# Moving all 32 low-half subtractions of the weight split to GpSimd in a scan-plus-experts kernel

## What is computed

```python
xn = _layernorm(x)
x = x + attn(xn, A, W_delta, delta_bias, W_B, W_C) + ffn(xn, W1, b1, W2, b2, Wr, br)
# attn: delta = softplus(xn W_delta + bias); per step of L = 2048, per (d, n) of 256 x 16:
#   h = exp(delta A) h + (exp(delta A) - 1) / A * B_t * x_t ;  y = sum_n h C_t
# ffn: 8 experts, the best 2 of each token: gelu(xn W1[e] + b1[e]) W2[e] + b2[e], weighted
```

## Time and profile before

| | |
|---|---|
| median of 3 runs | 1374.65 us (1370.88 to 1374.74) |
| the profiled execution's own time | 1372.12 us |
| its span, first to last instruction | 1370.4 us |
| mean granted TensorE clock | 0.949 |
| busy: PE, DVE, ACT, POOL | 1199.7, 1048.8, 860.1, 841.5 us |

### The profile page before, as it was taken

One profiled execution on the slowest core, in us unless ns is written; L12 is line 12 of the kernel. 1 busy time (PEld: TensorE's weight loads), 2 busy tenths in 40 slices (PEclk: granted clock), 3 DMA queues, 4 the chain that ended last, 5 costly groups with the idle time before them and its releaser, 6 DMA issues. The chain is left out here.

```text
span 1370.4 us, 22272 instructions
## 1 busy us (share of the span) xinstructions
PE 1199.7 (88%) x7674; PEld 734.0 (54%) x7674; DVE 1048.8 (77%) x1413; ACT 860.1 (63%) x1422; POOL 841.5 (61%) x603
## 2 busy tenths in 40 slices
PE   1567767566999989999999999999999999999896
PEld 0432323223566656666666666666666666666552
DVE  6865889885777877867777767778777787777878
ACT  3645666655577557586767666675776857676521
POOL 2628989861647556566565757666575666656552
PEclk9558898988999999999999999999999999999999
DMA  6596667664343343343442443434534334334324
GB/s 207 194 267 193 231 218 243 204 246 143 83 107 109 115 113 113 103 115 110 137 118 84 131 128 92 123 111 122 127 93 132 113 98 130 113 108 111 84 47 142
DMA packets 87386, 186.95 MB, mean 136 GB/s; under 512 B 12784, under 2 KB 64880, under 8 KB 77168
## 3 DMA queue, kind: packets, MB, share of 16 engines
q1 hardware_dynamic: 69280, 163.19, 36.4%
q0 software_dynamic: 18000, 22.42, 9.8%
HBM read 135.48 MB, written 57.96 MB: 141 GB/s over the span
## 5 line engine op out<-in xcount | busy, mean ns | idle before, releaser
L921 POOL TENSOR_TENSOR ax<-ax,x 128x512 f32<-128x512 f32 x256 | 335.4, 1313 | 387.7 <-ACT ax L821 386.2
L1134 PE MATMUL bank<-k_xT,k_WB 128*128 128x512 f16 x1536 | 390.7, 392 | 102.5 <-DVE hb L1024 92.4
L1011 DVE TENSOR_TENSOR bank<-ax,bank 128x512 f32<-128x512 f32 x256 | 177.5, 693 | 281.7 <-PE bank L1134 246.4
L1134 PE MATMUL bank<-k_xT,k_WC 128*128 128x512 f16 x1536 | 386.5, 389 | 0.8 <-DVE ysum L1045 0.8
L1134 PEld LDWEIGHTS bank<-k_xT,k_WB 128*128 128x128 f16 x1536 | 146.0, 100 | 269.6 <-DVE hb L1024 118.4
L1134 PEld LDWEIGHTS bank<-k_xT,k_WC 128*128 128x128 f16 x1536 | 154.0, 100 | 194.0 <-issue 20.6
L1024 DVE TENSOR_TENSOR_SCAN hb<-aexp,state,bank 128x512 f32<-128x512 f32 x192 | 243.9, 1270 | 0.0
L814 ACT ACTIVATE aexp<-k_dcur,k_A 128x512 f32<-128x512 f32 x256 | 180.7, 711 | 59.4 <-DVE hb L1024 54.9
L1183 PE MATMUL bank<-stage,k_x 128*128 128x256 f16 x1872 | 217.1, 273 | 0.0
L1183 PEld LDWEIGHTS bank<-stage,k_x 128*128 128x128 f16 x1872 | 183.2, 98 | 37.8
L1036 DVE SCALAR_TENSOR_TENSOR bank<-hb,k_rA,bank 128x512 f32<-128x512 f32 x240 | 179.1, 746 | 1.7
(11 more groups left out here) (139 smaller groups left out, 1223.9 us busy)
## 6 DMA issues: line engine op xcount, KB each, us to landing
k_x<-wsplit SPq DMA_DIRECT2D x78, 1024.0 KB, 4.7
stage<-in_W SPq DMA_DIRECT2D x32, 512.0 KB, 5.2
wsplit<-stage SPq DMA_DIRECT2D x32, 512.0 KB, 3.2
xs<-k_zero SPq DMA_DIRECT2D x1, 10140.0 KB, 44.5
stage<-xs SPq DMA_DIRECT2D x39, 260.0 KB, 5.3
stage<-in_b SPq DMA_DIRECT2D x39, 128.0 KB
k_x<-in_x SPq DMA_DIRECT2D x4, 1024.0 KB, 9.8
stB<-in_WBT SPq DMA_DIRECT2D x8, 512.0 KB, 4.7
```

Of the source, the lines that this page charges most:

```text
L921: nc.gpsimd.tensor_tensor(ax[:, g % MR], ax[:, g % MR], x32[:, hf], ALU.mult).then_inc(ax_done, 1)
L1011: v.tensor_tensor(bank, ax[:, g % MR], bank, ALU.mult).then_inc(ux_done, 1)
L1134: ins = mm(bank[:], W[:, a, kc, n, hf * P:(hf + 1) * P], xT[:, c, b, kc, :], start=(k == 1), stop=(k == 3 * KC))
```

## The change

DVE no longer subtracts. POOL's `low_piece` takes every k instead of the even ones, each in tile `piece_step(k) + 4`. For an odd piece that is one tile number later than DVE had it. The two semaphores for "low half done" become one, and SP waits for its count.

```diff
-    p_lo = [sem("p_lo_pool"), sem("p_lo_dve")]
+    p_lo = sem("p_lo")
...
             if k >= W_BUF:
-                sp.wait_ge(p_lo[k % 2], (k - W_BUF) // 2 + 1)
+                sp.wait_ge(p_lo, k - W_BUF + 1)
...
         def store_piece(k):
-            sp.wait_ge(p_lo[k % 2], k // 2 + 1)
+            sp.wait_ge(p_lo, k + 1)
...
             nc.gpsimd.tensor_tensor(whl[:, k % HL_BUF, 1, :], wst[:, k % W_BUF, :], whl[:, k % HL_BUF, 0, :],
-                                    ALU.subtract).then_inc(p_lo[0], 1)
+                                    ALU.subtract).then_inc(p_lo, 1)
...
-            for k in range(0, SPLITS, 2):
+            for k in range(SPLITS):
                 if piece_step(k) + 4 == g:
                     low_piece(k)
...
-        def low_piece(k):
-            dve.wait_ge(p_hi, k + 1)
-            v.tensor_tensor(whl[:, k % HL_BUF, 1, :], wst[:, k % W_BUF, :], whl[:, k % HL_BUF, 0, :],
-                            ALU.subtract).then_inc(p_lo[1], 1)
...
-            for k in range(1, SPLITS, 2):
-                if piece_step(k) + 3 == g:
-                    low_piece(k)
             hc_op(g)
```

## The result

| | before | after |
|---|---|---|
| median | 1374.7 us (1370.88 to 1375.65, 4 runs) | 1388.03 us (1387.57 to 1389.3, 4 runs) |
| profiled execution, its span | 1372.12, 1370.4 us | 1387.66, 1385.9 us |
| first scatter starts | 107.80 us | 109.41 us |
| subtraction of piece 30 starts | 287.92 us | 307.94 us |
| last subtraction ends | 298.61 us | 313.38 us |

The changed kernel takes 1.0104 times as long (95% interval 1.0083 to 1.0124): it is 13 us slower. The forecast was 1389 us.

A forecast was written before the change was run, and what follows sets the result against it. POOL was taken to bound the piece stage: 31.4 us added less 9.8 and 2.6 put piece 30 at 306.9 us and the stage end 13.8 us later. With 0.3 for stores, 14 us on 1374.65 gave 1389 us, range 1382 to 1402.

The forecast's parts named there:

- POOL leads the stage: From first scatter to last subtraction, POOL sets the pace until its subtraction of piece 30 at 287.92 us.
- Added, 15 x 2.09 = 31.4 us: On POOL before piece 30: odd pieces 1 to 29 add 15 subtractions at 2.09 us each, 31.4 us.
- Removed, the stretching of 12 scatters, 9.8 us: On POOL: 12 scatters lying over a DVE subtraction lose 0.82 us of stretching each, 9.8 us.
- Removed, the two waits, 2.6 us: On POOL: two waits for ACT of 1.3 us vanish, since one more subtraction lies ahead of the waiting one.
- The end: Behind piece 30 POOL does a product and piece 31; last low half at 312.4 us, stage ends 13.8 us later.
- The hand-over and the rest are rigid: After the last subtraction: PE's 17.2 us wait for slot rows moves along unchanged, as does the stretch behind it.
- DVE's 41 us buy nothing of their own: In the piece stage: the 41.0 us removed from DVE gain nothing themselves, since DVE then only follows POOL.
- The store chain is covered by 2.7 us: Store, landing and ACT's copy before a buffer's next subtraction: 4.5 us against POOL's 7.2; no cover at the end.
- Rival B: In the piece stage: scatters stay long, so the shift is 24 us, 1398 us; chance 0.10.
- C: Rival: POOL's subtraction without DVE's around costs 1.22 us, so the stage ends 16 us earlier, 1359 us; chance 0.04.
- A: Rival: the store chain takes over, POOL waiting for ACT's copy; 1402 us with ten waits of 1.3 us; chance 0.13.
- D: Rival: PE becomes the pacemaker in the stage under a lasting low clock; shift 31 us, 1406 us; chance 0.04.

The follow-up runs named there:

- e5: Changed kernel with the odd pieces' subtraction left out and their low halves stored as zeros; 1359.39 us, 0.9878 of the kernel before.
- e3: Changed kernel plus 16 extra DVE subtractions of two SBUF inputs where its own had been; 1389.89 us, 1.0119 of the kernel before.
- e4: Changed kernel plus 16 DVE maximum reductions over one SBUF input where its subtractions had been; 1387.28 us, 1.0102 of the kernel before.
- e1: All 32 subtractions on DVE, the even pieces one tile number earlier than POOL had them; 1359.54 us, 0.9895 of the kernel before.
- e6: Changed kernel with every piece stored twice and the buffer free only after both stores; 1391.44 us, 1.0106 of the kernel before.
- e7: Kernel before with its 16 odd subtractions still on DVE but one tile number later; 1389.47 us, 1.0104 of the kernel before.
- e10: Changed kernel with the odd pieces' subtractions on POOL one tile number earlier, where DVE had them; 1392.49 us, 1.0102 of the kernel before.

## Why the prediction was right

- **POOL leads the stage.** Right. After the change it has no wait for ACT, and e5 shows each subtraction at its full price on the path.
- **Added, 15 x 2.09 = 31.4 us.** Right: 2.08 us each (e5).
- **Removed, the stretching of 12 scatters, 9.8 us.** Right: the scatters' sum went from 73.0 us to 63.3. The cause is shown by e3 and e4; the prediction had not seen that the order of starts decides.
- **Removed, the two waits, 2.6 us.** Right, both gone.
- **Piece 30.** 199.1 us behind the first scatter by the sum, 198.5 measured. The 0.6 us left are at least in part products that DVE's subtraction had held: their mean fell from 1311 to 1280 ns.
- **The end.** The shift of the stage was 13.2 us for 13.8. The allowance of 0.3 us for the store chain was not needed. The median moved by 13.3 us for the 14 forecast; the two profiled executions differ by 15.5, because the first scatter started 1.6 us later, which the prediction had not counted.
- **The hand-over and the rest are rigid.** Right: 17.22 us against 17.21, and 0.7 us over the rest.
- **DVE's 41 us buy nothing of their own.** Right for this change, but the sentence hid the larger fact: a good part of the 41 us was waiting beside POOL's subtractions. Without those, in e1, a DVE subtraction takes 1494 ns, so 16 x 1.07 = 17 of the 41 us go with them; 32 took 47.8 us.
- **The store chain is covered by 2.7 us.** Held with POOL as the only subtracting engine, as far as tested: a landing 1.6 us later cost POOL 0.6 us (e6). With DVE following one tile later it is not (e7), so the cover belongs to the division and not to the buffers.

Rival B falls by the scatters and by e4, C by the 2131 ns, A by POOL's waits of zero. D falls by the windows: PE has 75 us to spare in the stage, at a clock of 0.92.

What stays open: why the first scatter starts at 107.8 us in one execution and at 114.4 in another, see the last section. The 0.7 us behind the hand-over is less than executions differ by.

## What to carry to other kernels

Moving work off an engine that looks as full as its neighbour needs the waits, not the busy shares: here POOL led with 89% and DVE followed with 86%, but 17 us of DVE's time went with POOL's subtractions beside its own. When two engines collide, give the whole of a job to the one that does it faster alone; in this kernel the division by halves paid on both sides, 9.8 us in POOL's scatters and 17 us in DVE's subtractions. And where a change moves an operation to another engine and to another place in the order, test the two apart in both directions.

## What the runs showed of the hardware

- A VectorE subtraction of two SBUF inputs took 1.22 us alone and 4.57 us with a GpSimd product and subtraction beside it. The longest took 8.58 us, at 310.78 us in e3, while GpSimd ran three products and two subtractions back to back. In all the traces 54 DVE subtractions took over 1.3 us, and each ended 1.08 to 1.09 us behind the last GpSimd instruction that had ended before it: from these cases, it had to wait until GpSimd paused or turned to a scatter.
- A scatter issue of GpSimd that starts while such a VectorE subtraction has 0.9 us or more to go takes 1.79 to 1.86 us instead of 0.99 (54 cases), and with 0.3 to 0.5 us to go 1.12 to 1.37 (10 cases). One that starts ahead of it keeps its time (54 of 54).
- A VectorE reduction with one SBUF input took 1.212 to 1.219 us in all 16 cases and stretched no scatter.
- The zeroing transfer of 10 MB, which gates the first scatter, landed after 44.5 us in the profile before and 46.1 after, and over all runs the first scatter started between 107.8 and 114.4 us. On the three chips of e1 to e10 it started at 109.5 to 110.4 us, 110.7 to 112.3 and 114.4, and the median of the kernel before was 1373.7, 1376.4 and 1378.7 us. That the one is the reason of the other was not tested.
